# SyncE issues the rows of the block four on ahead of the turned low half, in the single blocks of a routed expert layer

## The reference

```python
x = x + attn(layernorm(x))      # elu feature maps, a running sum of phi_k * v, an output projection
x = x + ffn(layernorm(x))
# ffn: 8 experts of width 512, the best 2 for each token, and a shared expert of width 1024
logits = x @ router_w;  top_logits, top_indices = top_k(logits, 2);  scores = softmax(top_logits)
for e in range(8):
    g, u = split(permuted * mask @ w1[e])          # rows sorted by expert
    out = out + where(mask, (silu(g) * u) @ w2[e], 0)
shared = silu(x @ w_gate) * (x @ w_up) @ w_down
return combined + shared
```

## Time and profile before

| | us |
|---|---|
| median of three executions | 347.97 |
| the profiled execution, its own time | 347.06 |
| its span, first to last instruction | 345.4 |
| PE busy in the span | 331.1 (96%) |
| DVE, ACT, POOL busy | 236.7, 203.4, 203.0 |
| share of PE in the chain that ended last | 81% |
| granted TensorE clock, mean | 0.996 |

### The profile page before, as it was taken

One profiled execution on the slowest core, in us unless ns is written; L12 is line 12 of the kernel. 1 busy time (PEld: TensorE's weight loads), 2 busy tenths in 40 slices (PEclk: granted clock), 3 DMA queues, 4 the chain that ended last, 5 costly groups with the idle time before them and its releaser, 6 DMA issues.

```text
span 345.4 us, 9507 instructions
## 1 busy us (share of the span) xinstructions
PE 331.1 (96%) x3104; PEld 275.7 (80%) x3104; DVE 236.7 (69%) x593; ACT 203.4 (59%) x370; POOL 203.0 (59%) x305
## 2 busy tenths in 40 slices
PE   7999998999999999999999899999999999999991
PEld 6779887888888898888988466666678888888880
DVE  4999989799889888787788755655553344433440
ACT  3679949696897977947527444544453334443340
POOL 4777566686885768747673743354453354346444
PEclk9999999999999999999999999999999999999998
DMA  6992151555684566625885346857966156544635
GB/s 194 392 356 51 24 134 27 134 150 186 141 240 92 138 192 136 194 83 157 243 258 153 76 99 83 106 76 87 104 98 74 35 66 88 63 63 62 63 37 58
DMA packets 65279, 43.31 MB, mean 125 GB/s; under 512 B 49104, under 2 KB 60368, under 8 KB 64848
## 3 DMA queue, kind: packets, MB, share of 16 engines
q1 hardware_dynamic: 51152, 32.19, 37.2%
q0 software_dynamic: 9392, 10.44, 19.2%
q10 hardware_dynamic: 4688, 0.07, 1.2%
HBM read 19.09 MB, written 12.90 MB: 93 GB/s over the span
## 4 chain that ended last, share of the span: by engine, by line
PE 81%; POOL 5%; issue 3%; DVE 3%; DMA 3%; SPq 2%; ACT 2%; POOLq 1%; DVEq 0%
PE bG L249 15%; PE bU L249 15%; PE bD L1057 9%; PE bG L1187 5%; PE bU L1187 5%; PE bV L1285 4%; PE bQ L1285 3%; PE bV L1208 3%; PE bQ L1208 3%; PE bV L249 3%; PE bQ L249 3%; PE bK L249 2%; PE bT L925 2%; PE bK L1164 1%; PE bT L945 1%
## 5 line engine op out<-in xcount | busy, mean ns | idle before, releaser
L1807 DVE SCALAR_TENSOR_TENSOR ab<-bU,sg 128x512 f32<-128x512 f32 (+1 forms) x63 | 43.2, 686 | 56.2 <-PE bU L249 39.5
L848 POOL DMA_INDIRECT out_y<-xs,dst_row x31 | 48.9, 1578 | 52.2 <-DVE dst_row L2171 26.7
L1442 ACT ACTIVATE sg<-bG 128x512 f32<-128x512 f32 x64 | 37.8, 590 | 43.7 <-PE bG L249 25.7
L609 POOL DMA_INDIRECT x_rows<-rows,slot_u x32 | 42.3, 1322 | 14.3 <-issue 14.3
L1607 ACT ACTIVATE ws_h<-ab 128x512 f16<-128x512 f32 (+1 forms) x35 | 21.8, 622 | 38.8 <-DVE ab L1807 38.5
L2138 DVE TENSOR_TENSOR ws_h<-ab,ws_h 128x512 f16<-128x512 f32 (+1 forms) x35 | 24.0, 685 | 20.3 <-ACT ws_h L1607 20.3
L1449 ACT ACTIVATE ah<-ab 128x512 f16<-128x512 f32 x32 | 20.1, 628 | 29.0 <-DVE ab L1807 28.8
L249 PE MATMUL bG<-work,we 128*128 128x256 f16 x240 | 29.5, 273 | 0.2 <-issue 0.2
L249 PE MATMUL bU<-work,we 128*128 128x256 f16 x240 | 29.5, 273 | 0.0
L249 PEld LDWEIGHTS bG<-work,we 128*128 x240 | 23.3, 98 | 3.3 <-issue 0.5
L249 PE MATMUL bG<-xT,ws_h 128*128 128x256 f16 x144 | 24.5, 273 | 1.2 <-ACT sg L1442 1.2
(11 more groups left out here) (379 smaller groups left out, 882.4 us busy)
## 6 DMA issues: line engine op xcount, KB each, us to landing
stage<-in_w_expert SPq DMA_DIRECT2D x24, 512.0 KB, 4.9
we<-in_w_shared SPq DMA_DIRECT2D x3, 1024.0 KB, 11.9
out_y<-xs SPq DMA_DIRECT2D x8, 256.0 KB, 2.5
xs<-bo POOLq DMA_DIRECT2D x7, 256.0 KB, 4.8
xs<-in_x SPq DMA_DIRECT2D x1, 1280.0 KB, 17.6
x_rows<-we SPq DMA_DIRECT2D x9, 134.0 KB
xs<-in_x SPq DMA_DIRECT2D x3, 256.0 KB, 4.1
work<-x_rows SPq DMA_TRANSPOSE x40, 3.4
```

The lines of the kernel that those rows point to most:

```text
L609: pool.indirect_dma_start(xrows, bass.IndirectOffsetOnAxis(ap=slot_u[q][:, k, t:t + 1], axis=0), rows2[q][:, t, :].bitcast(U16), None).the ...
L848: pool.indirect_dma_start(out_rows, bass.IndirectOffsetOnAxis(ap=dst_row[:, b:b + 1], axis=0), ya[b % NY], None, bounds_check=NT * P - 1, ...
L1442: act.activation(sg[q][:, 0:m], src[:, 0:m], ACT.Silu, scale=1.0 / WS).then_inc(S["sg_done"], 1)
L1807: dve.scalar_tensor_tensor(out=ab[q][:, 0:m], in0=src[:, 0:m], scalar=1.0 / WS, in1=sg[q][:, 0:m], op0=ALU.mult, op1=ALU.mult).then_inc(S[ ...
```

## The change

In each of the single blocks the call of `turn_low(b)` moves behind the calls of `load_rows` of the same step. Nothing is added or removed; buffers, waits and semaphores stay as they are. The pair blocks have no `turn_low`, so their steps are as before.

```diff
             for b in range(NBLK):
-                if b < NS:
-                    turn_low(b)
                 if b + NX - 1 in MIXED:
                     load_rows(b + NX - 1, 1)
                 if b + NX < NBLK:
                     load_rows(b + NX)
+                if b < NS:
+                    turn_low(b)
```

## The result

| | before | after |
|---|---|---|
| median of 20 executions, us | 347.23 | 348.19 |
| lowest and highest | 346.67, 348.81 | 347.06, 349.59 |
| ratio, with its 95% interval | | 1.0027 [1.0018, 1.0037] |
| the profiled execution, us | 347.06 | 349.53 |
| its span | 345.4 | 347.9 |

What follows compares the result with a forecast made beforehand. The prediction took TensorE, busy 96% of the span with no gap to make up a stall, as the bound; the larger stall, max(0.2, 1.1) = 1.1 us, on the mean of 347.5 gave 348.5 us, range 346.8 to 349.8.

Steps and rivals of the forecast that it cites:

- Sooner rows are worth 0, steps 2 to 15 cost 0: Later steps: rows start some 2.4 us sooner but TensorE never waited for them; cost of steps 4 to 15: 0.
- bound of 3.15 us for the issue of a pair: Mixed steps: two rows' DMAs take at most 3.15 us to issue, low half 0.75 us late, with 2.8 us to spare.
- The first steps: SyncE enters the loop late, at 197.60, all waits fulfilled; each DMA put ahead delays by its full issue time.
- The terms of the maximum: Stalls at the first two down products: the larger counts, max(0.2, 1.1) = 1.1 us.
- turned low half 0: Block 0: issued at 198.85 instead of 197.60, landing 3.6 us, use at 202.24, so 0.2 us late.
- turned low half 1: Block 1: issued at 202.8 or 203.85, landing 3.6 us, use at 206.36; late by 0.0 or 1.1, 1.1 taken.
- sign that the prediction gave for itself: TensorE idle at L1208 within the down product of block 1, perhaps one at block 0, none in any later one.
- The rule of the Trainium skill: Block 0: low half not read before the 128 rows ahead; there about 202, first term up to 0.2 us, sum unchanged.
- slot of 2.34 us at 200.19: SyncE's issue of turned low half 1 before, median 1.21; blamed on ScalarE's two small DMAs, so the pair takes 3.6 us.
- Slower by more: Rival, blocks 0 and 1: low halves behind rows land after 5.2 us, late by 1.8 and 2.7; 350.2 us; chance 0.11.
- Nothing happens: Rival, first steps: both low halves there on time, time as before, 347.0 to 348.0 us; chance 0.28.
- Faster: Rival, step 4 and later: silu sooner, stall of 0.2 us gone, 347.3 us; chance 0.03 for over 0.5%.

Runs made afterwards that it cites:

- step 2 on alone: Order of before in steps 0 and 1, the changed order from step 2 on, against the kernel before: 1.0003 [0.9994, 1.0012].
- step 0 alone: Turned low half behind the rows only in step 0, the other 15 steps as before, against the kernel before: 1.0035 [1.0021, 1.0050].
- second profile: The changed kernel run and profiled once more, nothing else changed, against the kernel before: 1.0021 [1.0004, 1.0038].
- shorter list of registers: Changed order with 6 instead of 12 row addresses loaded ahead of the loop, against the kernel before: 0.9995 [0.9987, 1.0004]; order of before with 6: 0.9996.
- 64 empty instructions: Changed order with 64 empty instructions at the start of TensorE's program, against the kernel before: 1.0022 [1.0009, 1.0035].

## Why the prediction was right, and where not

- **What bounds the kernel** (TensorE without a gap, so a stall goes through in full): right. Waits of 1.8 and 0.5 us at L1208 are in the ends of the two traces of the changed kernel (1.82 of 2.46, and 0.5 of 0.5).
- **Sooner rows are worth 0, steps 2 to 15 cost 0**: right, 1.0003 with step 2 on alone. The bound of 3.15 us for the issue of a pair was too low (4.03), and the low halves had the room for that too.
- **The first steps: each DMA put ahead is its full issue time of delay.** Right, and the core of it: step 0 alone is the whole loss, and 1.25 us less of backlog takes it away.
- **The terms of the maximum.** This is what was mis-sized. For turned low half 0 the prediction had a landing of 3.6 us and 0.2 us of stall; with a fetch in flight it took 3.65 to 5.24 us in six traces, and the wait was 0 to 1.8. For turned low half 1 it had 1.1; no trace has a wait there. In the second profile it is issued at 203.46, near the 203.85 of the prediction, but lands within 2.8 us, before its use at 206.37 + 0.87 = 207.24, which the first stall had moved back by 0.5. The sign that the prediction gave for itself, an idle time within the down product of block 1 and perhaps one at block 0, came the other way round. That the sum of 1.1 is near the measured 0.9 is therefore luck: the stall changed places, and neither term was right.
- **Why.** The prediction read the slot of 2.34 us at 200.19 as the price of ScalarE's DMAs and took it as fixed to that stretch, for the issue and the landing of whatever follows. It is nearly fixed in time, but what stands there is a fetch, and it hits what is in flight then: without ScalarE's DMAs the pair of rows still took 3.27 us. The DMA view of before, 200.2 to 200.3 us:

```profile
q8 instruction: 1, 0.02, 75.7%
```

  Before, it hit low half 1, which has 6.2 us from its issue to its use (200.19 to 206.36) and landed after 3.6. The change puts low half 0 there, which has 3.4 us. So both 1.25 us of delay and the stretched landing fell on the same transfer.
- **The rule of the Trainium skill**, *DMA: Bandwidth & Descriptors*, "Queues, rings and completion order" (descriptors of a queue are consumed in ring order): the traces don't speak against it, since low half 0 landed behind the rows of block 4 in all nine in which it stands there; but it has next to no price here. Right behind 128 rows it landed after 2.5 us where no fetch was in flight. The prediction's estimate by the rule, about 202, took 3.4 us for the landing of these rows, where seven of the nine traces have 2.7 to 2.8. With step 0 alone they took 4.5 and low half 0 came 0.4 us behind them; in that trace the order may have had a part.
- **The rivals.** "Slower by more" named a landing of 5.2 us, from standing right behind rows on one queue beside ScalarE's small packets; the landing of 5.24 came, in one trace of six, at low half 0 and not at 1, and its 1.8 us is just the price given for that term. The mechanism was another. "Nothing happens" is what the shorter list of registers makes of it. "Faster" isn't seen anywhere.

## What to carry to other kernels

Before moving one DMA ahead of another on an issuing engine, look at where that engine enters the loop: in steady state the swap was free for 14 steps, while at the entry, where all waits are already fulfilled, each DMA put ahead delays the rest by its full issue time. Compare the new issue time with the use of the *first* items, with the longest landing of any transfer of that kind in the trace, and not the median. Here the longest of the turned low halves before, 3.8 us, was still too short; the longest of the rows, 5.2, was what one trace then showed. A backlog made of small things (here 12 register loads and two saves ahead of the loop) decides whether the same order is free or not.

## What the runs showed of the hardware

The fetches of instructions, one 16 KB transfer each on a queue of their own kind (27 in a run, 12 us apart at the median, 7 to 19 at the ends), slow the transposing DMAs around them in the routed part. From the records of the 13 traces of this study, the DMAs of rows from block 4 on and the turned low halves: of 144 issues on SyncE that overlap a fetch in time, 70 took 1.5 us or more; of 532 that don't, 1 did (medians 1.46 and 1.20 us). Of the turned low halves whose completion records are all there, those in flight with a fetch landed after 3.9 us at the median (64, up to 5.35), the others after 2.9 (91, up to 4.3). A long landing also has more chance to meet a fetch, so these medians say somewhat too much; the nine traces of turned low half 0 above don't have that fault. In the part ahead of 185 us there is no such difference in the issues: 4 of 45 with a fetch took 1.5 us or more, and 24 of 267 without. So a fetch is not the only thing that makes a transposing DMA slow, and what it costs depends on what else is there.

A fetch itself took 0.9 to 1.8 us on its DMA engine. Its place goes by the instructions of TensorE that have a row in the trace: the one around 200 us starts when 3790 to 3808 of them have started, in all 13 traces, also with 32 matmuls and their weight loads fewer (205.4 us) or more (194.6 us). The 64 empty instructions didn't change that count. That a fetch holds up the share of a transposing DMA that falls to the same DMA engine is the likely way, but no run here shows it.
